# C products turned in 64-row halves, more B products by diagonals, and row moments moved between engines

## The reference

```python
n = layernorm(x)                                  # over 512 channels
xp = n @ x_proj_w.T                               # 64 ranks, 16 B, 16 C
delta = softplus(xp[..., :64] @ dt_proj_w.T + dt_proj_b)
h = exp(delta * A) * h + delta * B * n            # per channel and state, along 2048 steps
y = (h * C).sum(states) + n * D;   x = x + y
m = layernorm(x)
scale = max(abs(m).max(-1), 1e-6) / 127;  q = clip(round(m / scale), -128, 127)
out = x + (q @ weight_q.T) * scale * weight_scale + bias
```

## Time and profile before

| | us |
|---|---|
| median of 3 runs | 2764.41 |
| lowest, highest | 2761.62, 2764.93 |
| span of the profiled execution | 2760.5 |
| PE busy (products) | 2736.5 |
| DVE busy | 2705.4 |
| ACT busy | 2690.0 |
| POOL busy | 2691.9 |

### The profile page before, as it was taken

The page is one execution under the profiler, slowest core; times in us unless marked ns, Lnnn a source line. Parts: engine busy times, 40 slices in busy tenths (PEclk is TensorE's granted clock), DMA queues, the critical chain, the costliest instruction groups (busy, mean ns, idle before and its releaser), DMA issues.

```text
span 2760.5 us, 59331 instructions
## 1 busy us (share of the span) xinstructions
PE 2736.5 (99%) x22612; PEld 2519.7 (91%) x22612; DVE 2705.4 (98%) x2801; ACT 2690.0 (97%) x4927; POOL 2691.9 (98%) x981
## 2 busy tenths in 40 slices
PE   8999999999999999999999999999999999999998
PEld 7999999999999999999999999999999999999987
DVE  7999999999999999999999999999999999999987
ACT  8999999999999999999999999999999999999995
POOL 5899999999999999999999999999999999999998
PEclk9999999999999999999999999999999999999999
DMA  6345446355454454464554544544545535445452
GB/s 198 100 101 139 123 116 148 107 124 133 118 142 117 120 142 123 116 143 112 124 131 116 145 112 117 149 112 127 137 118 124 127 117 149 111 113 154 99 133 54
DMA packets 271654, 344.35 MB, mean 125 GB/s; under 512 B 174917, under 2 KB 174917, under 8 KB 251018
## 3 DMA queue, kind: packets, MB, share of 16 engines
q1 hardware_dynamic: 250538, 275.54, 34.0%
q0 software_dynamic: 20832, 65.02, 13.8%
HBM read 253.60 MB, written 103.16 MB: 129 GB/s over the span
## 4 chain that ended last, share of the span: by engine, by line
PE 97%; DVE 1%; ACT 1%; issue 0%; DMA 0%; SPq 0%; DVEq 0%; POOL 0%; ACTq 0%
PE Y L855 32%; PE PB L830 23%; PE PB L833 21%; PE Y L851 4%; PE PM L962 4%; PE PM L921 4%; PE PM L902 4%; PE PM L892 2%; PE PM L930 2%; DVE A L994 1%; PE PM L909 0%; ACT A L669 0%; ACT DB L688 0%; PE PM L872 0%; PE PM L879 0%
## 5 line engine op out<-in xcount | busy, mean ns | idle before, releaser
L604 POOL TENSOR_TENSOR A<-A,CB 128x2048 f32<-128x2048 f32 x511 | 2342.0, 4747 | 42.4 <-ACT CAR L676 40.9
L994 DVE TENSOR_TENSOR_SCAN A<-A,CAR,PB 128x512 f32<-128x512 f32 x1536 | 1828.9, 1260 | 9.9 <-ACT A L669 4.6
L669 ACT ACTIVATE A<-DEL,an 128x512 f32<-128x512 f32 x2048 | 1332.5, 713 | 6.3 <-PE Y L855 5.8
L855 PE MATMUL Y<-idf,A 128*128 128x128 f32 x8192 | 1085.1, 273 | 0.0
L855 PEld LDWEIGHTS Y<-idf,A 128*128 128x128 f32 x8192 | 932.7, 141 | 6.5 <-issue 0.5
L688 ACT ACTIVATE DB<-XN,BC 128x512 f32<-128x512 f32 x1344 | 891.7, 711 | 3.6 <-DVE XN L1024 3.6
L833 PE MATMUL PB<-idf,DB 128*128 128x128 f32 x5376 | 764.1, 273 | 8.4 <-DVE A L994 7.0
L830 PEld LDWEIGHTS PB<-DG,XN 128*128 128x128 f32 x5632 | 685.9, 192 | 70.8 <-issue 48.3
L830 PE MATMUL PB<-DG,XN 128*128 128x128 f32 x5632 | 726.7, 276 | 2.5 <-DVE A L994 2.4
L833 PEld LDWEIGHTS PB<-idf,DB 128*128 128x128 f32 x5376 | 621.7, 141 | 66.3 <-issue 39.5
L994 DVE TENSOR_TENSOR_SCAN A<-A,PB 128x512 f32<-128x512 f32 x512 | 584.8, 1201 | 12.5 <-PE PB L833 7.4
(11 more groups left out here) (94 smaller groups left out, 1407.0 us busy)
## 6 DMA issues: line engine op xcount, KB each, us to landing
CB<-c_rows SPq DMA_DIRECT2D x128, 1024.0 KB, 4.8
DG<-b_diag SPq DMA_DIRECT2D x192, 256.0 KB, 5.0
X<-in_x SPq DMA_DIRECT2D x31, 1024.0 KB, 7.3
out<-X SPq DMA_DIRECT2D x31, 1024.0 KB, 5.2
out<-bias_rows POOLq DMA_DIRECT2D x31, 1024.0 KB, 8.8
out<-C POOLq DMA_DIRECT2D x31, 1024.0 KB, 12.7
b_diag<-DG SPq DMA_DIRECT2D x2, 1536.0 KB, 10.7
b_diag<-BC SPq DMA_DIRECT2D x192, 2.0 KB, 5.4
```

What stands on the lines that cost most here:

```text
L604: gp.tensor_tensor(A[s % NA][:, :, :], A[s % NA][:, :, :], CB[:, s % (4 * NG), :].unsqueeze(1).broadcast_to([128, KB, L]), ALU.mult).then_ ...
L669: act.activation(A[s % NA][:, g, :], DEL[k % 2][:, g, :], ACT.Exp, scale=an[:, g, n:n + 1])\
L855: i = pe.matmul(Y[j][:, g * 128:(g + 1) * 128], A[s % NA][:, g, j * 128:(j + 1) * 128], idf[:, :], is_transpose=True, start=False, stop=(n ...
L994: dve.tensor_tensor_scan(A[s % NA][:, g, :], A[s % NA][:, g, :], PB[(4 * s + g) % NPB][:, :], init, ALU.mult, ALU.add).then_inc(s_scan, 1)
```

## The change

- The C products are turned in halves of 64 rows (here channels): each 128 x 128 turn becomes two, with 64 moving columns of the identity, written to two different PSUM banks; the D products likewise. `Y` becomes `YR`, and the gather becomes eight instructions of 128 x 256 that wait for pairs of row tiles. POOL adds the two halves' row sums (`sum2`), and the squares wait for that.
- 34 of 64 row tiles go by diagonals (`ROWS`), so ACT scales 30 instead of 42 a chunk; SP stores and loads nine diagonals instead of six.
- The first moments are taken on ACT: four sums (`sum1`) and four squares (`sq1`) replace DVE's statistics and aggregates. All four row tiles are normalised on POOL. The centring goes from POOL to ACT.
- The small steps of POOL go to DVE, mostly as instructions of one element per partition with per-partition scalars (`as2`, `as4`, `step`, `step2`).
- All due times are new (`PERIOD` is 10000 instead of 1000).

The diff, without the tables of due times, declarations and waits that only follow from it:

```diff
-    ROWS = {2: 4, 5: 4, 8: 4, 11: 4, 14: 4, 15: 2}
+    ROWS = {1: 4, 3: 4, 5: 4, 7: 4, 8: 2, 9: 4, 11: 4, 13: 4, 15: 4}
...
-        Y = [ps(f"Y{i}", [128, D]) for i in range(T)]
+        YR = ps("YR", [128, T // 2, 2, D])
+        Y = [YR[:, i // 2, i % 2, :] for i in range(T)]
...
# POOL
-            def shift0(p):
-                gp.tensor_tensor(SM[:, 3, :], SM[:, 2, :], SM[:, 1, :], ALU.mult).then_inc(s_sh, 1)
             def xn_p(p, i):
-                j = NXA + i
-                gp.tensor_scalar(XN[p % 2][:, j, :], X[p % NX][:, j, :], SM[:, 2, j:j + 1], SM[:, 3, j:j + 1],
-                                 ALU.mult, ALU.add).then_inc(s_xnp, 1)
+                gp.tensor_scalar(XN[p % 2][:, i, :], X[p % NX][:, i, :], SM[:, 1, i:i + 1], SM[:, 2, i:i + 1],
+                                 ALU.add, ALU.mult).then_inc(s_xnp, 1)
-            def ascale(p):
-                gp.tensor_tensor(PW[:, 3, :], PW[:, 1, :], RO[:, 3, :], ALU.mult).then_inc(s_qu, 1)
-                gp.tensor_tensor(RO[:, 1, :], PW[:, 3, :], RO[:, 2, :], ALU.add).then_inc(s_as, 1)
-                gp.tensor_tensor(AM[:, 0, :], RO[:, 0, :], RO[:, 1, :], ALU.mult).then_inc(s_z, 1)
-                gp.tensor_scalar(AM[:, 1, :], AM[:, 0, :], 2e-6 * D, 1.0 / (254.0 * D), ALU.max, ALU.mult).then_inc(s_zm, 1)
-            def step(p):
-                gp.tensor_tensor(AM[:, 3, :], AM[:, 2, :], RO[:, 0, :], ALU.mult).then_inc(s_st, 1)
-            def centre(p, j):
-                gp.tensor_scalar(CQ[:, j * D:(j + 1) * D], X[p % NX][:, j, :], SX[:, 1, j:j + 1], AM[:, 3, j:j + 1],
-                                 ALU.add, ALU.mult).then_inc(s_c, 1)
+            def sum2(p):
+                gp.wait_ge(s_y, 2 * T * (p + 1))
+                gp.tensor_tensor(SX[:, 0, :], SY[:, 0, :], SY[:, 1, :], ALU.add).then_inc(s_sum, 1)
# ACT
+            def sum1(p, j):
+                act.activation(XN[p % 2][:, j, :], X[p % NX][:, j, :], ACT.Copy, accum_out=L1[:, 0, j:j + 1]).then_inc(s_s1, 1)
+            def sq1(p, j):
+                act.wait_ge(s_s1, T * p + j + 1)
+                act.activation(XN[p % 2][:, j, :], X[p % NX][:, j, :], ACT.Square, bias=L1[:, 0, j:j + 1], scale=-float(D),
+                               accum_out=L1[:, 1, j:j + 1]).then_inc(s_s2, 1)
             def square(p, j):
-                act.wait_ge(s_y, T * p + j + 1)
                 if j == 0:
+                    act.wait_ge(s_sum, p + 1)
-            def xn(p, j):
-                act.activation(XN[p % 2][:, j, :], X[p % NX][:, j, :], ACT.Identity, bias=SM[:, 3, j:j + 1],
-                               scale=SM[:, 2, j:j + 1]).then_inc(s_xn, 1)
+            def centre(p, j):
+                act.activation(CQ[:, j * D:(j + 1) * D], X[p % NX][:, j, :], ACT.Identity, bias=AM[:, 0, j:j + 1],
+                               scale=AM[:, 3, j:j + 1]).then_inc(s_c, 1)
# PE
             def th(k, i):
+                at = [[YR[:, j // 2, r, 256 * (j % 2) + 64 * g:256 * (j % 2) + 64 * g + 64] for r in range(2)] for g in range(KB)]
+                half = [slice(64 * r, 64 * r + 64) for r in range(2)]
...
                     for g in range(KB):
-                      i = pe.matmul(Y[j][:, g * 128:(g + 1) * 128], XT[:, g, j * 128:(j + 1) * 128], dd[:, g, :],
-                                    start=(g == 0), stop=False, skip_group_check=True)
+                        for r in range(2):
+                            i = pe.matmul(at[g][r], XT[half[r], g, j * 128:(j + 1) * 128], dd[half[r], g, half[r]],
+                                          start=(g == 0 and j % 2 == 0), stop=False, skip_group_check=True)
...
                 for g in range(KB):
-                    i = pe.matmul(Y[j][:, g * 128:(g + 1) * 128], A[s % NA][:, g, j * 128:(j + 1) * 128], idf[:, :],
-                                  is_transpose=True, start=False, stop=(n == NS - 1), skip_group_check=True)
+                    for r in range(2):
+                        i = pe.matmul(at[g][r], A[s % NA][half[r], g, j * 128:(j + 1) * 128], idf[half[r], half[r]],
+                                      is_transpose=True, start=False, stop=(n == NS - 1), skip_group_check=True)
# DVE
-            def gather(p, j):
-                dve.wait_ge(s_th, 4 * NS * (p + 1) - 3 + j)
-                dve.scalar_tensor_tensor(X[p % NX][:, j, :], Y[j][:, :], 1.0, X[p % NX][:, j, :], ALU.mult, ALU.add,
-                                         accum_out=SX[:, 0, j:j + 1]).then_inc(s_y, 1)
-            def stats(p, j):
-                dve.bn_stats(ST[:, j, :], X[p % NX][:, j, :]).then_inc(s_bn, 1)
-            def aggr(p):
-                for i in range(T):
-                    dve.bn_aggr(MV[:, i, :], ST[:, i, :]).then_inc(s_ag, 1)
+            def gather(p, i):
+                j, r = divmod(i, 2)
+                if r == 0:
+                    dve.wait_ge(s_th, 4 * NS * (p + 1) - 3 + (j | 1))
+                channels = X[p % NX][:, j, :].rearrange("p (g r c) -> p r g c", g=KB, r=2)[:, r, :, :]
+                dve.scalar_tensor_tensor(channels, YR[:, j // 2, r, 256 * (j % 2):256 * (j % 2) + 256]
+                                         .rearrange("p (g c) -> p g c", g=KB), 1.0, channels, ALU.mult, ALU.add,
+                                         accum_out=SY[:, r, j:j + 1]).then_inc(s_y, 1)
+            def as2(p):
+                for j in range(T):
+                    i = dve.tensor_scalar(RO[:, 1, j:j + 1], PW[:, 1, j:j + 1], RO[:, 3, j:j + 1], RO[:, 2, j:j + 1],
+                                          ALU.mult, ALU.add)
+            def as4(p):
+                for j in range(T):
+                    i = dve.tensor_scalar(AM[:, 0, j:j + 1], RO[:, 1, j:j + 1], RO[:, 0, j:j + 1], 2e-6 * D,
+                                          ALU.mult, ALU.max)
+                i.then_inc(s_z, 1)
+                dve.wait_ge(s_z, p + 1)
+                dve.tensor_scalar(AM[:, 1, :], AM[:, 0, :], 1.0 / (254.0 * D), 1.0, ALU.mult, ALU.mult).then_inc(s_zm, 1)
+            def step(p):
+                for j in range(T):
+                    i = dve.tensor_scalar(AM[:, 3, j:j + 1], AM[:, 2, j:j + 1], RO[:, 0, j:j + 1], 1.0, ALU.mult, ALU.mult)
+            def step2(p):
+                for j in range(T):
+                    i = dve.tensor_scalar(AM[:, 0, j:j + 1], AM[:, 3, j:j + 1], SX[:, 1, j:j + 1], 1.0, ALU.mult, ALU.mult)
```

More of the change, by code:

```diff
@@ L3 @@
 from contextlib import ExitStack
-PERIOD = 1000
+PERIOD = 10000
 PLACES = {
[L8 to L60, removed]
[8 rows of a table removed]
[L69 to L80, removed]
@@ new lines @@
+        10099),
+        "centre": (16943, 17042, 17167, 18369),
+        "d_t": (-4027, -3406, -3268, -3069),
+        "decay": (-674, -441, -191, 4, 56, 59, 301, 301, 377, 555, 875, 1274, 1400, 1561, 1802, 2164, 2234,
[3 rows of a table added]
+        "delta": (-3184, -2993, -2726, -1662),
+        "dl_t": (-2659, -2020, -1632, -1061),
+        "du": (-2395, -1438, -271, -11),
+        "gather": (12842, 12854, 12890, 12940, 12960, 12997, 12997, 13050),
+        "idle": (200000, 200001, 200002, 200003),
+        "inv": (14917,),
@@ new lines @@
+        "qt_out": (19171, 21728, 24760, 25298),
+        "root": (14783,),
+        "rstd0": (-7658,),
+        "scale_a": (19878, 20256, 20521, 20987),
+        "scale_out": (200000, 200001, 200002, 200003),
+        "scale_p": (17341,),
+        "scales": (16446,),
+        "scan": (1458, 1835, 2189, 2206, 2357, 2436, 2449, 2458, 2511, 2537, 2555, 2597, 2824, 2945, 3418, 3647,
[4 rows of a table added]
+        "square": (13518, 13590, 13637, 13716),
+        "step": (16961,),
+        "step2": (17088,),
+        "store_c": (-4477,),
@@ L105 @@
[L105 to L131, removed]
[9 rows of a table removed]
-        "times_c": (-21597, -13312, -6626, -3345, -3345, -2638, -1549, 169, 491, 494, 514, 514, 514, 530,
-        602, 759),
-        "turn": (1723,),
-        "var1": (1355,),
-        "warm": (-25231, -24121, -23794, -23737, -22003, -21960, -15900, -15080, -13326, -13116, -12141,
@@ new lines @@
+        "qt_out": (19365, 20411, 21421, 22195),
+        "root": (14564,),
+        "rstd0": (-60784,),
+        "scale_a": (20028, 20175, 20476, 20871),
+        "scale_p": (18209,),
+        "scales": (16491,),
+        "scan": (2167, 2167, 2452, 2505, 2505, 2505, 2592, 2682, 2722, 3397, 3439, 3565, 3578, 3578, 3578, 3582,
[4 rows of a table added]
+        "square": (12679, 13709, 13748, 13938),
+        "step": (16610,),
+        "step2": (17097,),
+        "store_c": (-59553,),
+        "store_g": (-64766,),
[11 rows of a table added]
+        "times_c": (-1709, -1423, 1552, 1864, 1880, 2750, 2775, 3186, 3186, 3188, 3705, 4171, 4736, 5526, 5559,
@@ L186 @@
[L186 to L187 removed]
[8 rows of a table removed]
[L196 to L198 removed]
+        "act_b": (-912, -906, -495, -270, -140, -48, 234, 546, 649, 952, 1013, 1254, 1364, 1386, 1486, 1489,
+        1520, 1712, 1922, 1929, 2218, 3325, 6049, 6716, 6783, 7403, 7526, 7653, 7901, 7937),
+        "amax": (11927,),
```

(26 more changed lines are left out.)

277 lines of the change are left out of this document (145 added, 132 removed), and 82 rows, old and new, of tables (FIRST, LAST, PLACES).

## The result

The changed kernel takes 2912.8 us (median of 4 runs, 2911.0 to 2913.2) against 2763.0 of before beside it (2760.7 to 2764.9): ratio 1.0539, 95% interval 1.0524 to 1.0554, 150 us slower. I had forecast 2768 and a range up to 2850.

A forecast was written before the change was run, and what follows sets the result against it. Four engines (DVE, ACT, POOL, PE) were taken to bound within half a microsecond a chunk, DVE alone after the change at 84.4 us: 2764.4 + 32 x (84.4 - 84.46) + 6 = 2768 us, range 2720 to 2850.

The forecast's parts named there:

- DVE's sum: DVE's demand a chunk: statistics and aggregates go, half gathers and 17 small steps come; net +0.1, to 84.2 us.
- rival B: DVE's 128 x 4 multiply waits for POOL's product, 2.3 us on average: 71 us more, 2839 (2780 to 2900); chance 0.22.
- Turns in halves: On PE, the two 64-row halves of a turn run side by side, 0.055 us a pair, saving 14.0 us a chunk.
- Rival C: On PE the halves don't overlap: 2937 us at least, 3050 in the middle, near 3900 at worst; chance 0.12.
- Switches: On PE, 46 changes a chunk between 64-row turns and whole products cost 0 to 7.6 us; 3.8 taken.
- the sum that I gave by it: PE's demand a chunk if a change of tiling mode drains TensorE: 83.5 us, still below DVE.
- ACT, POOL and DVE: Demand a chunk after the change: ACT 83.0 us (net -1.0), POOL 82.1 (net -1.8 to -2.1), DVE 84.2 (net +0.1).
- rival A: DVE's small steps cost 0.066 us each and all four engines fall: 2733 us (2720 to 2750); chance 0.30.
- a second engine on the chain: Sign of a wrong forecast: an engine besides DVE stays on the chain, where DVE alone was to set the period.
- The ends: Head about 3 us lost to moments on ACT; tail +3 with squares waiting for halves and sum: +6 us together.
- A 128 x 4 TENSOR_SCALAR on DVE with a mean over 1 us is B: Sign to look for in the profile: such a mean for this step on DVE would show rival B, the wait for POOL.

The follow-up runs named there:

- the fused form: The changed kernel with its 16 single-column steps and the 128 x 4 multiply written as six scalar_tensor_tensor of 128 x 4: 2984.94 us, ratio 1.0813.
- the version with single columns: The changed kernel with its 128 x 4 multiply by a constant on DVE made as four steps of 128 x 1: 2793.95 us, ratio 1.0108.
- the one step moved alone: The kernel before with only the last of POOL's four small steps (maximum and multiply, 128 x 4) moved to DVE: 2788.57 us, ratio 1.0090.

## Why the prediction was wrong

**The step that failed is a term of DVE's sum: the 128 x 4 multiply, taken at 0.066 us, lasted 3.9 us on average, because it waited for POOL's products.** That cost 119 of the 150 us. The prediction had this as its rival B, and had B's chance (0.22) and its size too low. The cast's row had shown the mechanism, and I set it aside with "four elements may not take the form that waits", without a row that spoke for that. The runs show that two columns wait too, and four in each of the three forms tried. The size was wrong too: 2.3 us, half of one product, assumes a step issued anywhere in a product that gets in when that product ends. The 23 that did get in waited 2.9 us on average, and eight waited for the next whole product too (7.2 to 8.3), so the mean was 3.9. B's sum of 71 us should have been 119, and its upper end (2900) lay below the result.

The Trainium skill speaks for B more plainly than I had used it. By its page SBUF — State Buffer (SBUF: two separate sides), the port pair that DVE and GpSimd share is an exclusive lock for a whole instruction, taken by DVE in a two-port mode, or with two SBUF inputs against a GpSimd operation that reads SBUF. By its page VectorE: DVE Perf Modes (What auto-detection actually checks), a single source and a destination in SBUF, with even outermost dimensions, are enough for such a mode; no size is said to be too small. The runs agree for two and four columns (2.04 and 3.9 us), for two tensors (3.9) and for the fused form (4.86), and one column doesn't wait (0.146). The page has the blocked one wait for one whole instruction, and doesn't say that it may lose to the next as well, as eight steps did here. My theory for the fused form went against that rule and fell.

**Turns in halves: right in kind.** 40 halves take 1.46 us at 0.228 for one. The group, and PE's timeline in the changed kernel:

```profile
L860 PE MATMUL YR<-idf,A 64*128 64x64 f32 x16384 | 681.1, 228 | 0.0
```

```profile
1399.29 2.94 PE L831 MATMUL PB<-DG,XN 128*128 128x128 f32 x24
1402.17 0.71 PE L860 MATMUL YR<-idf,A 64*128 64x64 f32 x16
1402.81 0.71 PE L831 MATMUL PB<-DG,XN 128*128 128x128 f32 x4
...
1409.09 1.46 PE L860 MATMUL YR<-idf,A 64*128 64x64 f32 x40
1410.47 0.71 PE L831 MATMUL PB<-DG,XN 128*128 128x128 f32 x4
```

(1.46 - 0.228)/39 = 0.0316 each, 0.063 a pair; I took 0.055 (bounds 0.055 and 0.109 or more), so the turns cost 256 x 0.008 = 2 us a chunk more than forecast. Rival C is out.

**Switches: at the dear end.** 24 products last 2.88 us from start to start, 0.19 beyond 24 x 0.112; 16 halves last 0.64, 0.14 beyond 8 x 0.063, and 40 halves 1.38, 0.12 beyond 20 x 0.063. So 46 changes cost 23 x (0.19 + 0.13) = 7.4 us, where I took 3.8 of 0 to 7.6. Whole turns need 2929.7 - 2794.0 = 136 us more, a period of some 89.3; less 256 x (0.109 - 0.063) = 11.8 and with the switches PE comes to 84.9, where its busy share gives 795.30/800 x 85.04 = 84.5. I had 79.7, inside my bounds. The Trainium skill (TensorEngine Tiling (Array Packing), Key Properties) says that a change of tiling mode drains TensorE; these gaps agree, and the sum that I gave by it, 83.5, was the nearer one. PE was freed much less than forecast.

**ACT, POOL and DVE: right.** From the version with single columns: ACT 782.20/800 x 85.04 = 83.1 (forecast 83.0), POOL 82.1 (82.1), DVE 84.4 (84.2; that version has three small instructions more). In the changed kernel the steps with two scalars per partition stand (0.79 - 0.262)/3 = 0.18 apart, as taken (0.186), and those with one (0.55 - 0.2)/3 = 0.12 (0.126). So rival A (0.066 each) is out by its own row. Half gathers stand 0.345 apart (0.35).

**The period without the wait.** 85.04 against 84.4: 0.6 us a chunk, 19 to 20 us in all. DVE idles 0.6 us a chunk, not 0.2, and PE, at 84.5, stands as high as DVE; the chain of that version is 94% PE. So the sign that I had named for a wrong forecast, a second engine on the chain, holds for this version as well. That two engines are near their limit together fits this, but no run takes one of them away without other harm, so it stays argued.

**The ends.** +6 forecast, some 10 measured. The first scan starts at 36.42 us against 26.76 before. PE's turn for it, in the changed kernel:

```profile
26.97 8.90 PE L884 MATMUL PM<-idf 128*128 128x128 f32 x80
35.71 1.47 PE L834 MATMUL PB<-idf,DB 128*128 128x128 f32 x12
```

I had the 3 us of moments on ACT (PE's first turn of normalised rows starts at 13.50 us, for 10.71 before), and overlooked that the new orders put 80 warming turns in one block ahead of the first B products. To drop them gains nothing, since the products then run at half the pace and the diagonals arrive at 37.5. So about 7 us of the head are in the order of loads and warming together; which load is to come earlier wasn't tried.

**The signs that I had named.** "A 128 x 4 TENSOR_SCALAR on DVE with a mean over 1 us is B" came, at 3.9.

## What to carry to other kernels

Before a small step moves to DVE, look at what POOL runs there: with products of 4.6 us back to back, a DVE multiply of two or four columns that reads SBUF alone can wait to the end of the running product, and of the next one too where that follows at once (8.3 us at most here). It holds up all that is queued behind it on DVE. Cut to single columns, the same arithmetic took 119 us less. If the trace of before shows a form waiting even once, price even the smallest step of that kind at up to the other engine's whole instruction, unless a row shows it not to wait: of 4.6 us it cost 3.9 on average in one place, and 1.0 in the other, where POOL had to wait for its result. And an engine's gain from finer tiles is to be set off against each switch between tilings, at 0.1 to 0.2 us here.

## What the runs showed of the hardware

- DVE waiting for POOL: 128 x 4 by a constant 3.9 us on average (0.17 to 8.3), with two tensors 3.9, fused 4.9 at the head of a group, 128 x 2 waits too; three columns weren't tried. Not waiting under the same products: single columns (0.14 to 0.26), the 128 x 4 reciprocal (0.15), the reduction of 128 x 2048 (2.26), scans and gathers with an operand in PSUM. Why the reciprocal passes isn't explained by any run.
- In the changed kernel a step that waits misses the gap between two products where that is 0.13 to 0.42 us, even when POOL issues a DMA there (1414.10 to 1414.52), and gets in where it is 0.87 or more. One that starts with a product loses to it (five times with the fused forms).
- Turns of 64 rows in pairs: 0.063 us a pair, with loads of 140 ns each; all 16384 loads are busy 584 us, where 8192 of twice the rows were busy 933.
- TensorE's granted clock in the steady stretch: 1.00 with single columns, and with the one step moved alone (waits of 1.0 us); 0.98 in the changed kernel, where PE waits up to 7.3 us at a time for DVE, and 0.96 with the fused forms.
